# Trainium2 kernel study: W1 stores and W2 splits moved inside the order of a three-block transformer kernel

## Time and profile before

| | |
|---|---|
| median of 3 runs | 1499.03 us (1497.62 to 1499.47) |
| the profiled execution: own time | 1496.73 us |
| its span | 1494.9 us |
| PE busy | 1472.9 us |
| DVE, ACT, POOL busy | 940.5, 669.4, 625.4 us |
| HBM traffic | 155 GB/s over the span |

### The profile page before, as it was taken

How to read it: one execution, slowest core, us unless ns; L and a number is a source line. 1 busy time by engine, 2 the same in 40 slices (tenths; PEclk the granted TensorE clock), 3 DMA queues, 4 the chain that set the end, 5 groups by cost and what they waited for, 6 DMA issues and landing times. The chain is left out here.

```text
span 1494.9 us, 24228 instructions
## 1 busy us (share of the span) xinstructions
PE 1472.9 (99%) x8712; PEld 1196.9 (80%) x8712; DVE 940.5 (63%) x1878; ACT 669.4 (45%) x2023; POOL 625.4 (42%) x544
## 2 busy tenths in 40 slices
PE   8999999999999999998999999999999999999999
PEld 5888888888888668777888778888888888888887
DVE  6677777777776677777767653764357434764354
ACT  4656555565644455555766433432224223432210
POOL 6756667676654447665856112301114102401001
PEclk9999999999999999999999999999999999999999
DMA  7222232222215435687554765535553554545342
GB/s 256 68 90 81 79 99 72 103 76 79 78 57 165 175 120 162 235 283 257 192 183 142 269 228 185 177 136 199 201 183 117 214 190 169 176 155 200 146 133 93
DMA packets 92919, 232.57 MB, mean 156 GB/s; under 512 B 9792, under 2 KB 17984, under 8 KB 87680
## 3 DMA queue, kind: packets, MB, share of 16 engines
q1 hardware_dynamic: 92128, 230.92, 44.6%
q10 hardware_dynamic: 672, 0.10, 0.0%
HBM read 174.17 MB, written 56.82 MB: 155 GB/s over the span
## 5 line engine op out<-in xcount | busy, mean ns | idle before, releaser
L1326 ACT ACTIVATE pa<-bank,neg_max 128x128 f32<-128x128 f32 x512 | 181.2, 408 | 136.5 <-DVE neg_max L1720 136.5
L724 PE MATMUL bank<-w_hi,g_hi 128*128 128x512 f32 x512 | 200.5, 392 | 0.0
L726 PE MATMUL bank<-w_hi,g_lo 128*128 128x512 f32 x512 | 199.3, 389 | 0.0
L725 PE MATMUL bank<-w_lo,g_hi 128*128 128x512 f32 x512 | 199.3, 389 | 0.0
L1218 PE MATMUL bank<-op_hi,ring 128*128 128x512 f32 x448 | 175.0, 391 | 2.5 <-DVE u2p L2140 1.4
L1222 PE MATMUL bank<-op_hi,ring 128*128 128x512 f32 x448 | 174.3, 389 | 0.0
L1220 PE MATMUL bank<-op_lo,ring 128*128 128x512 f32 x448 | 174.3, 389 | 0.0
L2278 POOL TENSOR_TENSOR xrc<-xrc,b 128x512 f32<-128x512 f32 x32 | 50.1, 1598 | 275.2 <-DMA xrc<-x_dram 275.2
L2306 POOL TENSOR_TENSOR pa<-pa,rec 128x512 f32<-128x512 f32 x128 | 142.8, 1125 | 51.9 <-DVE rec L1743 51.8
L1573 ACT ACTIVATE sum<-sum,cols 128x512 f32<-128x512 f32 x128 | 92.0, 722 | 112.6 <-DVE sum L2140 112.6
L1326 ACT ACTIVATION_READ_ACCUMULATOR pa<-bank,neg_max 128x1 f32 x512 | 126.9, 248 | 0.0
(11 more groups left out here) (263 smaller groups left out, 3553.6 us busy)
## 6 DMA issues: line engine op xcount, KB each, us to landing
ring<-w_dram SPq DMA_DIRECT2D x32, 1792.0 KB, 7.6
rows<-st_dram SPq DMA_DIRECT2D x32, 512.0 KB, 4.7
hid_dram<-sum SPq DMA_DIRECT2D x64, 256.0 KB, 2.2
hid<-hid_dram SPq DMA_DIRECT2D x64, 256.0 KB, 2.7
w_dram<-w_parts SPq DMA_DIRECT2D x8, 1792.0 KB, 7.4
xa<-xt_in SPq DMA_DIRECT2D x32, 256.0 KB, 4.2
xra<-xt_in SPq DMA_DIRECT2D x32, 256.0 KB, 2.8
x_dram<-h SPq DMA_DIRECT2D x32, 256.0 KB, 2.0
```

Source lines behind the costliest of these rows:

```text
L724: nc.tensor.matmul(dst, w_hi, a_hi, start=start, stop=False)
L725: nc.tensor.matmul(dst, w_hi, a_lo, start=False, stop=False)
L726: return nc.tensor.matmul(dst, w_lo, a_hi, start=False, stop=stop)
L1326: last = nc.scalar.activation(pa[:, j, m, :], scores_bank[j][:, m * P:(m + 1) * P], ACT.Exp, bias=neg_max[:, j * C + m:j * C + m + 1], acc ...
```

## The change

- SP stores the first W1 piece of a group right after the group's first residual store, and the second where both were before.
- ACT rounds the second W1 piece of a group after the two squares instead of before them.
- `t_first` gets four buffers; POOL runs all four `rest_first` together, ahead of the last `add_bias`, and waits for the query biases (whose rows the larger buffer overlaps) instead of for `low_first`.
- In group 7 DVE takes `norm_low_b` of b = 3 after the row maximum of b = 3; `low_first(0)` stays in the group, the other three follow `copy_ptb` of the last sequence.
- W2: nothing is split at p = 0; piece 0 is split in p = 1, pieces 1 and 2 at the end of p = 1, 3 and 4 at the end of p = 2, 5 and 6 at the end of p = 3, 7 at the end of p = 4. The loads of pieces 2 and 3 are issued in p = 1, of 4 and 5 in p = 2, of 6 and 7 in p = 3.

```diff
 def w2_pieces(p):
-    return ((), (0,)) if p == 0 else ((1,), ()) if p == 1 else ((2 * p - 2,), (2 * p - 1,)) if p < 5 else ((), ())
+    return (((), ()), ((0,), (1, 2)), ((), (3, 4)), ((), (5, 6)), ((), (7,)))[p] if p < 5 else ((), ())
...
-        t_first = at("t_first", [P, 2, 3, 2, P], F32, stage_w1_at)
+        t_first = at("t_first", [P, GB, 3, 2, P], F32, stage_w1_at)
...
                 store_x2(g, 0)
+                for i in w1_pieces(g)[:1]:
+                    store_w1(i)
                 store_x2(g, 1)
...
                 store_x2(g, 2)
-                for i in w1_pieces(g):
+                for i in w1_pieces(g)[1:]:
                     store_w1(i)
...
-                    if first and p < 4:
-                        for i in ((2,), (3,), (4, 5), (6, 7))[p]:
+                    if first and 1 <= p < 4:
+                        for i in ((2, 3), (4, 5), (6, 7))[p - 1]:
                             load_w2(i)
...
-                for i in w1_pieces(g):
+                for i in w1_pieces(g)[:1]:
                     split_w1(i)
                 squares_b(g + 1, 2)
                 squares_b(g + 1, 3)
+                for i in w1_pieces(g)[1:]:
+                    split_w1(i)
...
-                    if b < GB - 1:
+                    if b < GB - 1 or last:
                         norm_low_b(g + 1, b)
...
-                    if b == GB - 2:
+                    if b == GB - 2 and not last:
                         norm_low_b(g + 1, GB - 1)
...
-                    if last and 0 < b < GB - 1:
-                        low_first(b - 1)
+                    if last and b == 1:
+                        low_first(0)
...
                     copy_ptb(NG - 1, GB - 1)
-                    low_first(GB - 2)
-                    low_first(GB - 1)
+                    for b in range(1, GB):
+                        low_first(b)
...
                 pool.wait_ge(nb_free_act, GB * (NG - 1) + b + 3)
-                wait(pool, op_lo_made, GB + b - 1)
+                pool.wait_ge(rq_made, NB - GB)
...
                 for b in range(2, GB):
-                    if last:
-                        rest_first(b - 2)
                     if late_group(b) == g or late_group(b - 2) == g:
                         t3_late(b if late_group(b) == g else b - 2)
+                    if last and b == GB - 1:
+                        for i in range(GB):
+                            rest_first(i)
                     add_bias(GB * g + b, b, xrb, cb1, bxr_in[b], loaded(g + 1), bxr)
...
-                if last:
-                    rest_first(2)
-                    rest_first(3)
```

More of the change, by code:

```diff
@@ L1479, in round_first @@
                 act.wait_ge(t_made, GB + b + 1)
-                nc.scalar.activation(op_hi[:, T1:N4 + 1, :, b * P:(b + 1) * P], t_first[:, b % 2], ACT.Identity)\
+                nc.scalar.activation(op_hi[:, T1:N4 + 1, :, b * P:(b + 1) * P], t_first[:, b], ACT.Identity)\
                     .then_inc(op_hi_made, 1)
@@ L2023, in low_first @@
                 dve.wait_ge(op_hi_made, GB + b + 1)
-                low_half(op_lo[:, T1:N4 + 1, :, own], t_first[:, b % 2], op_hi[:, T1:N4 + 1, :, own])\
+                low_half(op_lo[:, T1:N4 + 1, :, own], t_first[:, b], op_hi[:, T1:N4 + 1, :, own])\
                     .then_inc(op_lo_made, 1)
@@ L2372, in rest_first @@
                 own = slice(b * P, (b + 1) * P)
-                t1, t2, n4 = (t_first[:, b % 2, v] for v in range(3))
+                t1, t2, n4 = (t_first[:, b, v] for v in range(3))
                 pool.wait_ge(nb_free_act, GB * (NG - 1) + b + 3)
-                wait(pool, op_lo_made, GB + b - 1)
+                pool.wait_ge(rq_made, NB - GB)
                 then(combine(t1, h_late[:, 0:2, own], hb_new[:, 0:2, own]))
```

## The result

The changed kernel takes 1508.24 us in the median of 4 runs (1505.24 to 1509.12), against 1499.25 us before: a ratio of 1.0054, with a 95% interval of 1.0041 to 1.0066. It is slower by about 8 us, where +3.2 was forecast. The profiled execution is the fastest of the four (1505.24 us, span 1503.4), so its comparison with the profiled execution of before (span 1494.9) shows 8.5 us.

The account below looks back on a forecast made before the run. TensorE matmuls bound the kernel (1472.9 of 1494.9 us). Second block -10.0, passage -0.4 and third block +13.6 sum to +3.2 us; added to the median of 1499.03 this gives 1502.2 us, range 1495 to 1508.

Parts of the forecast that it names:

- the cause of the old waits: Second block: the store of the piece two before is late; PE's waits for `tb` total 6.9 us.
- group 4: Second block: the earlier store removes its wait; 30.7 us against 35.80, 5.1 us won.
- the W2 price: Third block: late W2 loads make PE wait for ACT's bank copy three times, together 11.6 us.
- The sum for the clock: Third block: slow clock from three new standstills, 1.4 us each, 4.3 in all; bounds 0 and 5.1.
- the rival in which the clock holds: Third block: waits of 3 to 4 us leave the granted clock at 1.0; 1497.9 us, not slower; chance 0.14.
- the passage: Passage to third block: one wait goes, a new one of about 0.9 us comes; -0.4 us, bounds -1.9 and +1.
- I take 12.5 for groups 2 and 3 as well: Second block: squares end 12.5 us into groups 2 and 3, as in group 1; new wait about 1.0 us.
- equally close: Second block: DVE's row maximum, done by about 16.8 us into the group, is as close as the exponential.
- the clock in group 2: Second block: the old 3.4 us at 1.2 GHz, at most 1.7 us of loss, goes; none at 636 or 708.
- the second block gives less: Second block: slower DVE beside POOL doubles the new wait in three groups, +3 to 4 us; 1506 us; chance 0.14.
- The queue rival: Third block: later `xrc` loads do not delay the load ahead; step 1's wait 3.0, not 4.4; 1500.5 us; chance 0.16.

Follow-up runs that it names:

- The early store alone: Kernel before with only the early store of a group's first W1 piece, ACT's order untouched: 1486.57 us, ratio 0.9906.
- W2 loads first: Changed kernel with SP issuing the W2 loads ahead of the ring load and of the wait for the step's products: 1490.35 us, ratio 0.9931.
- W2 part alone: Kernel before with only the change's W2 splits and loads: 1512.88 us, ratio 1.0088.
- ACT's order alone: Kernel before with only ACT's second W1 rounding moved behind the squares: 1508.73 us, ratio 1.0057.
- the passage alone: Kernel before with only the four `t_first` buffers and the order of POOL and DVE in group 7: ratio 1.0001.

## Why the prediction was right or wrong

The direction was right, and the measured time stands at the upper end of the stated range: the ratio of 1.0054 on the prediction's 1499.03 gives 1507.1 us, 8.1 above before, against a bound of 1508; the median of its own runs, 1508.24, is 0.24 us past it. The size was too small by 5 us, and the case's own range of 1499.5 to 1505.5 was missed. The wide range held by its width and not by the sum: the second block came out 6.2 us dearer than forecast and the untouched first block 0.9, while the third block was 1.6 us cheaper.

- **Right: the cause of the old waits, and group 4.** The late store held ACT, DVE and PE in turn. Group 4 took 30.83 us; 30.7 was forecast. The early store alone wins 14 us (11 to 17) by its ratio, where its theory gave it 11.
- **Right: the W2 price.** The waits for the bank copy were forecast at 4.4, 3.9 and 3.3 us, 11.6 in all, and were 3.61, 2.79 and 3.76, 10.2 in all. Piece 2 landed after 7.4 and 8.4 us, and not after the 9.0 taken. ACT stood 7.73, 6.92 and 7.88 us ahead of these roundings, longer than the 4 to 7 us given as a sign. Two of the three waits were followed by a half-clock stretch: steps 2 and 4 took 20.5 and 20.6 us, step 3 took 18.0. The sum for the clock was taken at 4.3 us and was about 3.4, half of two stretches of 3.4 us. So the rival in which the clock holds, and which asked for two of three, failed by one.
- **Right: the passage, at nothing.** -0.4 us forecast; its part of the -0.79 us in the table, less the 0.25 us stop of step 1, is about -0.5, and alone it is 1.0001. The first `up` product waited 1.15 us, as the text had it in kind (0.9).
- **Wrong: "I take 12.5 for groups 2 and 3 as well".** This is the step that failed. The squares ended 13.8 us into group 2 and 13.9 into group 3, because the loads of `xb` still had one store of 1792 KB ahead of them and landed after 5.8 us in the median, where group 1's took 4.0 before. The run with that store moved behind them shows it: they landed after 2.9 us, and the squares ended 11.9 us into group 2. The text named that store and did not price it. Group 1 of the changed kernel has no such store, and its squares too ended later than forecast, 13.1 us in; its loads were issued 0.4 us later than before and landed after 4.2 to 4.4 us, and why stays open. The row of the exponential was 2.84 us behind `next_h` instead of 2.59, for DVE's row maximum came last (it ended at 645.32, the exponential began at 645.36): "equally close" was in fact just behind. So the wait was 1.7, 2.4 and 2.5 us in groups 1 to 3, where 1.0 was taken for each, with 2 as its upper bound. The text also read only the waits for `tb`, and left out the 1.78 us for `pb` that group 3 had already.
- **Wrong: the clock in group 2.** Around the end of the 2.37 us wait there the granted clock was 0.50 for 3.4 us, which the sum had left out for waits of 1 us. Group 2 won nothing at all. No stretch was left at 636 or 708, as forecast; in the third block there were two, from 854 and from 891.5 us, where the text had three places between 855 and 885.
- **The rival that came nearest** is "the second block gives less", 1506 us. Its place was right; its mechanism, a slower DVE beside POOL, is not what the runs show: DVE's row maximum cost 0.25 us of the group 2 wait.
- **The queue rival.** The landings do not decide it. Of the two sets of loads with `xrc` behind them the one at 0.5 us landed after 10.6 us at most, that at 3.4 us after 8.4; steps 2 and 3 of the changed kernel, with no `xrc`, had 7.5 and 8.2, the last hardly less than 8.4. By the Trainium skill, DMA: Bandwidth & Descriptors, section on queues, rings and completion order, descriptors of one ring are consumed in order on an engine, and by that alone the `xrc` loads would cost nothing; no run here took only the `xrc` loads away, so this stays open.

What I missed beyond the sizes was a question: where does ACT sit idle? In groups 2 and 3 of before it sits idle for a store, ahead of the first rounding. But group 1, which has no such store, shows what is next: both roundings are done by 599, and then ACT is idle until `xb` is there.

```profile
604.26 0.63 ACT L1352 ACTIVATE junk<-xb 128x512 bf16<-128x512 f32 x1 [5.31 <-issue]
```

With the store out of the way the loads of `xb` are the next bound in groups 2 and 3 too, and then what stands behind them in ACT's order is on the path.

## What to carry to other kernels

When a wait is taken off an in-order engine, look for the instruction that now waits longest on it, and keep independent work ahead of that one: here the same 1.8 us of rounding, in three groups, cost 10 us more behind the squares than ahead of them, clock included. A small load that is issued behind a bulk transfer should be asked for that much earlier, or be put ahead of it: here the W2 pieces took 7 to 8 us behind a 1792 KB load and mostly 3 us ahead of it, and the order of these DMA issues was worth 15 us of the profile to the change. Parts of a change that was put together should be timed apart, since a win of some 14 us and losses of 10 and 13 can hide in a sum of +8.

## What the runs showed of the hardware that had not been expected

The granted clock falls to 0.50, the 1.2 GHz level, behind short standstills of PE, and their length alone does not decide it. Waits of 1.85 us (before), 2.37 us (changed) and 2.60 us (W2 loads first) came with a stretch of 3.4 us at that level, and so did those of 3.61 and 3.76 us (changed). Waits of 1.78 us (before, twice), 2.54 and 2.79 us (changed), 2.58 us (W2 loads first) and 3.21 us (W2 part alone) did not. Nor did one of 3.47 us (ACT's order alone), though 3.31 us before and 3.44 us in the passage alone did; the matmuls behind it follow each other at the full rate, 0.23 us apart:

```profile
718.84 0.50 PE L724 MATMUL bank<-wvp_hi,hb_hi 128*128 128x512 f32 x1 [3.47 <-DVE tb L2032]
719.18 0.39 PE L725 MATMUL bank<-wvp_lo,hb_hi 128*128 128x512 f32 x1
```

What else decides it, these runs do not show. A forecast can thus give such a wait only a chance of a slow stretch, at up to 1.7 us of loss for each 3.4 us.

In the kernels with no wait above 1.3 us in these two blocks the mean granted clock of the span was 1.0, and their runs lie within 1.2 us of each other (1483.15 to 1484.27, 1482.61 to 1483.45), where those of the changed kernel spread over 3.9 us with clocks of 0.994 to 0.996. With the standstills most of the spread went as well, as far as four runs of each can tell.
